# Context, logits, routing weights and maxima turned in 32x32 blocks by VectorE and laid out by DMA

## The chip, the cores and the metric

One core of a Trainium2 chip (trn2) runs the whole program. The metric is the device time of one execution in microseconds; lower is better. Engines are named as the profile names them: PE is TensorE (PEld its weight loads), DVE is VectorE, ACT is ScalarE, POOL is GpSimd, SP is SyncE, which here issues every DMA.

## What is computed

The layer is a residual sum of an attention branch and a routed mixer branch over `x` of shape 8 x 1024 x 256, both fed by the same layer norm:

```python
xn = _layernorm(x)
x = x + attn(xn) + ffn(xn)
# attn: 16 heads of 16; heads 0..3 causal over all keys, heads 4..15 causal over a window of 64
scores = einsum('bhqd,bhkd->bhqk', q, k) * HEAD_DIM ** -0.5
ctx = einsum('bhqk,bhkd->bhqd', softmax(masked scores), v) ; attn = ctx @ w_out + b_out
# ffn: two branches (fwd and inverse) of 8 experts of rank 64
prod = einsum('btd,kdr->btkr', Q, V) * cumsum(einsum('btd,kdr->btkr', K, W), axis=1)
h = gelu(Q @ router_w1.T + router_b1); logits = h @ router_w2.T + router_b2 + expert_bias
weights = softmax(logits)
out = (einsum('btkr,kdr->btd', prod * weights[..., None], U) + weights @ b) / n_valid
ffn = (fwd + alpha_bi * inv) @ W_O.T
```

## The kernel before

**Chunks.** The 8 sequences are cut into 16 chunks of 512 tokens (`C`), two for each sequence; a chunk with an even number is the first half of its sequence and has fewer key tiles in the global heads. For every chunk a list of stages is written out by hand (`plan.stages`), and each of the five engine programs walks the same list in the same order and does its part of each stage. So every engine and SP's queue are strictly in the order of the list, and a stage that waits on one engine holds up all that stands behind it there. Nothing is scheduled at run time. The eight PSUM banks are handed out by turns: a stage on PE waits with `take` until the last user's contents have been read (`bank_read`).

**One chunk** goes through three phases on PE:
- *experts and peaks*: for each of 8 expert pairs `x` (xV), `c` (the cumulated yW), `product`, `mix` (into banks 0 and 1), woven with `lpeak` and `gpeak`: the raw scores, of which DVE takes the row maxima in 128-wide blocks (`peak`, `block_peak`). `found` splits the maxima in three bf16 parts, `rows` turns them on PE, ACT copies them (`peak_f`), SP writes them to DRAM and reads them back as three extra rows under the queries `QS`. `open` starts banks 0 and 1 with the bias rows times the routing weights `WT`; it comes right after the second expert pair's `c`.
- *local*: `lscore` and `lav` for the local heads in three groups of four (`grp` 1 to 3), woven with the next chunk's `turn` (token transpose, split in XH and XL), `sums`, and `parts` (the K and Q projections of the next chunk). For `parts` ACT writes the first bf16 part and DVE the other two (L1256, L1259, L1261). Then four `hidden` stages (the router's first layer, Gelu on ACT, banks 2 and 3 in turn).
- *global*: `gscore` and `gav` for the four global heads, woven with the next chunk's first `x` and `c`, `logits`, `gates`, `gate_parts`, `norm`, `values`; then `weight_rows`, two more `x`, and `finish`, the output projection into banks 0 and 1.

**What is turned on PE now.** `lav` and `gav` leave the context with channels on partitions, one extra row being the softmax sum. For each group ACT copies the bank (`cin`, L1125), PE turns it (`cout`, L913), DVE divides (L1375, L1377) into `ctok`; after the last group PE turns `ctok` back (`cparts`, L922), ACT and DVE split it in `PH` (L1131) and `PL` (L1384), and `finish` multiplies. The logits are copied by ACT (L1043), turned on PE (`gates`, L728), softmaxed by DVE; the weights go to DRAM and come back broadcast (`weights_d`, `wide`), and their three bf16 parts (`wstack`) are turned on PE (`weight_rows`, L737) and copied by ACT into `WT` (L1056).

Of the kernel before, what the change touches and what calls it, by code (L numbers as in the profile page):

```python
# [12 lines left out]
P = 128  # L13
# [56 lines left out]
def mixer_layer(  # L70
# [19 lines left out]
    HALF = C // 2  # L90
    HE_SLOTS = 6
# [14 lines left out]
    VW = HD + 1  # L106

# [73 lines left out]
    def add_cout(ch, grp):  # L181
        add("cout", ch, grp, uses=["bank4", f"craw{grp % 2}"])
# [13 lines left out]
    def add_lav(ch, grp, half):  # L196
        add("lav", ch, grp, half, uses=["bank7"] if half == 0 else [])
        where["lav", ch, grp, half] = [where["lscore", ch, grp, half, pair][1] for pair in range(2)]
        if half == 1:
            add("cin", ch, grp)  # L200
# [4 lines left out]
    def add_gav(ch, j, half):  # L205
        add("gav", ch, j, half, uses=["bank4"] if (j, half) == (0, 0) else [])
        where["gav", ch, j, half] = [where["gscore", ch, j, half, pair][1] for pair in range(2)]
        if (j, half) == tiles(ch % NC)[-1]:
            add("cin", ch, 0)
# [15 lines left out]
    def local_groups(ch):  # L225
# [4 lines left out]
        for n, (grp, half) in enumerate(units):  # L230
# [5 lines left out]
            if n > 2 and half:  # L236
                order[-1].append((add_cout, ch, grp - 1))
# [24 lines left out]
    def add_finish(ch):  # L262
        add("finish", ch, uses=["phl0", "phl1"])
# [24 lines left out]
    def add_gates(ch):  # L288
        add("gates", ch, uses=["bank7"])

    def add_rows(ch, which):
        add("rows", ch, which, uses=["bank4"])
# [67 lines left out]
    add("logits", 0, uses=["bank7", "craw0"])  # L360
# [3 lines left out]
    add("gates", 0, uses=["bank7"])  # L364
# [8 lines left out]
    add("weight_rows", 0, uses=["bank7"])  # L373
    add_open(0)

    for ch in range(CHUNKS):
# [4 lines left out]
        run(experts[0] + peaks[0])  # L381
        weave(experts[1:split], peaks[1:])
# [26 lines left out]
        if nxt:  # L409
            first_x, first_c = ([(add, ch + 1, 0, part) for part in range(2)] for add in (add_x, add_c))  # L410
            run(first_x + order[0] + first_c)
            add("logits", ch + 1, uses=["bank7", "craw0"])
# [14 lines left out]
        for k in range(DB):  # L427
            add_on("cparts", ch, k, uses=[score_use()])
# [3 lines left out]
        add_finish(ch)  # L432

    ctx = ExitStack()
    with ctx:
# [22 lines left out]
        l_bias = sb("l_bias", [P, 2])  # L458
        inv_n = sb("inv_n", [P, ST])
# [25 lines left out]
        weights_t = sb("weights_t", [P, T * 32])  # L485
# [10 lines left out]
        gate = sb("gate", [P, 4, T, 2 * KE])  # L496
        gsum = sb("gsum", [P, 4, T * 2])
        wstack = sb("wstack", [P, T, KSTK], BF16)
# [4 lines left out]
        positions = sb("positions", [P, ST], I32)  # L503
        peak = sb("peak", [P, T, NH])
        peak_rest = sb("peak_rest", [P, T, NH])
        block_peak = [sb(f"block_peak{c}", [P, T, NG, (c + 1) * T]) for c in range(NC)]
        peak_t = [sb(f"peak_t_{n}", [P, T, 3 * k], BF16) for n, k in (("local", NL), ("global", NG))]
        peak_f = sb("peak_f", [3 * NL, C], BF16)
        craw = sb("craw", [P, 2, C])
        ctok = sb("ctok", [P, T, D])  # L510
        cinv = sb("cinv", [P, 2, T, 4])
        logit_f = craw[:, 0, :]
# [4 lines left out]
        weights_d = nc.dram_tensor("weights_d", (2 * KE, C), F32, kind="Internal").ap()  # L517
        xr = x.rearrange("n (c t p) d -> n c p t d", c=NC, t=T)
# [5 lines left out]
        def raw(shape):  # L524
# [7 lines left out]
        rU = [t_[:, :, :].rearrange("p t d -> p (t d)").rearrange("p (b k) -> p b k", b=DB) for t_ in (xt, ctok)]  # L532
# [10 lines left out]
                [[WT[0:1, 0:D], WT[0:1, D:2 * D], peak_f[0:1, 0:D]]]  # L543

        def column(k):
# [12 lines left out]
        craw_read = [sem(f"craw{i}_read") for i in range(2)]  # L558
# [4 lines left out]
        peak_turned = [sem(f"peak_turned{i}") for i in range(2)]  # L563
# [6 lines left out]
        logits_ps, gate_max, gate_exp, gate_split, gate_turned = (sem(n) for n in ("logits_ps", "gate_max", "gate_exp", "gate_split", "gate_turned"))  # L570
# [4 lines left out]
            sem(n) for n in ("lpeaks_ps", "gpeaks_ps", "lscores_ps", "gscores_ps", "ctx_turned", "ctx_hi", "out_ps"))  # L575
        dve_step, pool_step, blank, cleared, selected, readied = (sem(n) for n in ("dve_step", "pool_step", "blank", "cleared", "selected", "readied"))
# [14 lines left out]
        N_RAW = [11, 5, 8, 5, 1]  # L591
# [62 lines left out]
        def tensor_program(e):  # L654
# [12 lines left out]
            for stage in plan.stages:  # L667
# [47 lines left out]
                elif kind == "logits":  # L715
# [3 lines left out]
                    for j in range(2 * DB):  # L719
                        k = where["hidden", ch, j][1]  # L720
                        e.matmul(PS[32 * j:32 * j + KE, 7, :], W2[:, j % DB, :], HE[:, k, :], start=True, stop=True,
                                 skip_group_check=True).then_inc(he_read[k])

                elif kind == "gates":
                    ch, = key
                    take(7, *stage)
                    for t in range(T):
                        ins = e.transpose(psum(7, lo=t * P, hi=(t + 1) * P), logit_f[:, t * P:(t + 1) * P], ident[:, :])  # L728
                    ins.then_inc(craw_read[0])

                elif kind == "weight_rows":
                    ch, = key
# [991 lines left out]
```

## Time and profile before

| | us |
|---|---|
| median of 3 runs (lowest, highest) | 1515.61 (1514.74, 1518.65) |
| profiled execution, its own time | 1516.97 |
| its span in the trace | 1515.3 |
| mean granted TensorE clock, share of full | 0.996 |
| PE busy | 1425.3 (94%) |
| DVE busy | 882.5 (58%) |
| ACT busy | 852.4 (56%) |
| POOL busy | 575.5 (38%) |

The profile is read from PE: it is busy in nearly every slice, so a microsecond taken from its instruction stream is a microsecond of the span, unless PE then waits for something. The trace repeats with the pair of chunks, some 180 us; times in it are given from the span's start.

### The profile page before, as it was taken

What the parts mean: (1) busy time and instruction counts of PE and PEld (TensorE: products, weight loads), DVE (VectorE), ACT (ScalarE), POOL (GpSimd) and SP (SyncE); (2) the same over time, 40 slices, a digit from 0 to 9 for tenths busy, and PEclk for the clock granted to TensorE, in tenths of its full rate; (3) what the DMA queues carried; (4) which work ended last, traced back from release to release, by engine and by line L of the source; (5) the groups of instructions that cost most, each with busy time, mean ns of one, the idle gap of its engine ahead of it and who ended that gap; (6) DMA issues with size and microseconds to landing.
All of it is one profiled execution on the core that took longest, in us unless ns stands there. A gap on an engine that the chain in (4) does not pass through costs nothing.

```text
span 1515.3 us, 36826 instructions
## 1 busy us (share of the span) xinstructions
PE 1425.3 (94%) x14977; PEld 1072.4 (71%) x14977; DVE 882.5 (58%) x1935; ACT 852.4 (56%) x1512; POOL 575.5 (38%) x663
## 2 busy tenths in 40 slices
PE   5999999999999999999999999999999999999997
PEld 4577775867758686686857777586775868678673
DVE  6676773556645675465755577356664567546451
ACT  3446557474665547565474645647466563756544
POOL 1044351444425343352424435143442524335241
PEclk9999999999999999999999999999999999999999
DMA  9322507253251625317053350615325162531600
GB/s 226 81 77 75 145 23 170 65 121 118 64 144 32 156 82 120 102 39 187 31 141 96 83 144 30 162 60 121 118 73 136 32 165 73 120 102 40 174 30 15
DMA packets 153789, 150.56 MB, mean 99 GB/s; under 512 B 28468, under 2 KB 136885, under 8 KB 153573
## 3 DMA queue, kind: packets, MB, share of 16 engines
q1 hardware_dynamic: 153620, 148.22, 37.7%
q8 instruction: 118, 1.93, 0.5%
q14 instruction: 51, 0.41, 0.1%
HBM read 106.98 MB, written 34.87 MB: 94 GB/s over the span
## 4 chain that ended last, share of the span: by engine, by line
PE 75%; DVE 11%; ACT 8%; issue 5%; POOL 1%; DMA 0%; ACTq 0%; POOLq 0%; DVEq 0%
PE PS L660 35%; PE PS L781 11%; PE PS L815 3%; PE PS L932 3%; PE PS L801 3%; PE PS L901 3%; PE PS L869 3%; PE PS L883 3%; ACT HE L1116 2%; PE PS L913 2%; PE PS L987 2%; PE PS L845 2%; ACT HE L1108 2%; DVE block_peak L1292 2%; DVE PL L1384 1%
## 5 line engine op out<-in xcount | busy, mean ns | idle before, releaser
L1547 POOL TENSOR_TENSOR PL<-prod,PH 128x512 fp32r<-128x512 f32 x128 | 164.7, 1287 | 215.1 <-ACT PH L1078 215.1
L1542 POOL TENSOR_TENSOR prod<-prod,rest 128x512 f32<-128x512 f32 x96 | 123.3, 1287 | 265.1 <-ACT prod L1068 146.0
L660 PE MATMUL PS<-XH,WH 128*128 128x512 f32 x512 | 218.3, 426 | 4.5 <-DVE XL L1232 1.9
L1292 DVE TENSOR_REDUCE block_peak<-PS 128x4 f32<-128x512 f32 x288 | 181.0, 684 | 54.2 <-PE PS L815 54.2
L660 PE MATMUL PS<-XL,WH 128*128 128x512 f32 x512 | 203.7, 398 | 0.0
L660 PE MATMUL PS<-XH,WL 128*128 128x512 f32 x512 | 203.2, 397 | 0.0
L1078 ACT ACTIVATE PH<-prod 128x512 fp32r<-128x512 f32 x128 | 80.8, 631 | 209.6 <-DVE prod L1365 209.5
L1525 POOL TENSOR_SCALAR_AFFINE_SELECT HE<-HE 128x256 f32<-128x256 f32 x128 | 51.0, 411 | 347.9 <-ACT HE L1116 345.3
L1116 ACT ACTIVATE HE<-PS 128x512 f32<-128x512 f32 (+1 forms) x320 | 159.7, 552 | 24.8 <-PE PS L883 22.6
L1068 ACT ACTIVATE prod<-PS 128x512 f32<-128x512 f32 x128 | 76.1, 594 | 125.3 <-PE PS L660 114.9
L1285 DVE TENSOR_REDUCE peak<-PS 128x4 f32<-128x512 f32 x192 | 120.6, 682 | 41.1 <-PE PS L801 41.1
L1365 DVE TENSOR_TENSOR prod<-PS,prod 128x512 f32<-128x512 f32 x128 | 88.2, 689 | 87.8 <-PE PS L660 85.1
L781 PE MATMUL PS<-UH,PH 128*128 128x256 f32 x512 | 132.2, 293 | 0.0
L781 PE MATMUL PS<-UL,PH 128*128 128x256 f32 x512 | 125.5, 279 | 0.0
L660 PEld LDWEIGHTS PS<-XH,WH 128*128 128x128 f32 x512 | 96.9, 189 | 29.3 <-DVE rest L1256 3.6
L660 PEld LDWEIGHTS PS<-XH,WL 128*128 128x128 f32 x512 | 96.7, 189 | 23.4
L660 PE MATMUL PS<-CH,WH 128*128 128x512 f32 x256 | 108.9, 425 | 0.7 <-DVE prod L1365 0.7
L1108 ACT ACTIVATE HE<-PS 128x512 f32<-128x512 f32 x192 | 103.4, 591 | 10.5 <-PE PS L845 10.5
L660 PEld LDWEIGHTS PS<-XL,WH 128*128 128x128 f32 x512 | 97.3, 190 | 14.3
L883 PEld LDWEIGHTS PS<-area 99*128 99x128 bf16 x640 | 41.4, 97 | 93.0 <-ACT HE L1116 55.8
L883 PE MATMUL PS<-area 99*128 99x256 bf16 (+1 forms) x640 | 99.6, 265 | 8.1 <-ACT HE L1116 3.9
L660 PE MATMUL PS<-CH,WL 128*128 128x512 f32 x256 | 101.8, 398 | 0.0
(196 smaller groups left out, 3142.3 us busy)
## 6 DMA issues: line engine op xcount, KB each, us to landing
parts_d<-area SPq DMA_DIRECT2D x32, 768.0 KB, 5.1
area<-parts_d SPq DMA_DIRECT2D x128, 192.0 KB, 8.4
rest<-weights_d SPq DMA_DIRECT2D x192, 128.0 KB, 2.9
area<-parts_d SPq DMA_DIRECT2D x32, 576.0 KB, 8.4
tok<-in_L_attn_x_dram SPq DMA_DIRECT2D x16, 512.0 KB, 6.3
xt<-in_L_attn_x_dram SPq DMA_DIRECT2D x16, 512.0 KB, 4.2
wide<-weights_d SPq DMA_DIRECT2D x64, 128.0 KB, 3.0
out_dram<-xt SPq DMA_DIRECT2D x16, 512.0 KB, 3.7
```

What stands on the lines that cost most here:

```text
L660: ins = e.matmul(ps, a, b, start=first and k == 0, stop=last and k == n - 1, skip_group_check=True)
L781: ins = e.matmul(out_half(t), (PH, PL)[part][:, h, t * P:(t + 1) * P], u[:, j, :], start=False, stop=False, skip_group_check=True)
L883: ins = e.matmul(psum(i, lo=HALF * a + lo, hi=HALF * (a + 1)), KG[0:KSTK, g, j * P:(j + 1) * P], QS[0:KSTK, g, half * HALF + lo:(half + 1) ...
L1068: e.activation(prod[:, j % 3, :], psum(2), ACT.Copy).then_inc(bank_read[2])
L1078: e.activation(PH[:, h, :], prod[:, j % 3, :], ACT.Copy).then_inc(phi)
L1108: e.activation(HE[:, k, :], psum(i), ACT.Exp, scale=SCALE).then_inc(bank_read[i])
L1116: e.activation(two(HE[:, k, :], lo), two(psum(i), lo), ACT.Exp, scale=SCALE).then_inc(bank_read[i])
L1285: e.tensor_reduce(peak[:, t, NG + 4 * grp:NG + 4 * (grp + 1)], psum(i).rearrange("p (a k) -> p a k", a=4), AX_X, ALU.max).then_inc(bank_re ...
L1292: e.tensor_reduce(block_peak[ch % NC][:, t, :, j], psum(i).rearrange("p (a k) -> p a k", a=4), AX_X, ALU.max).then_inc(bank_read[i])
L1365: e.tensor_tensor(prod[:, r, :], psum(3), prod[:, r, :], ALU.mult).then_inc(bank_read[3])
L1542: e.tensor_tensor(prod[:, j % 3, :], prod[:, j % 3, :], wide[j % WIDE], ALU.mult).then_inc(weighed)
L1547: e.tensor_tensor(PL[:, j % 2, :], prod[:, j % 3, :], PH[:, j % 2, :].bitcast(F32), ALU.subtract).then_inc(plo)
```

## The change

No operand of the main stream is turned on PE any more. DVE turns 32x32 blocks in place (`e.transpose`); what has to move between partition groups moves by DMA, or is absorbed in the order of weight rows.
- *Context*: `cin`, `cout` and `cparts` go. DVE turns the bank itself into `craw` (new stage `ctx`), divides into `ctok` (still in blocks), and turns `ctok` back (`cturn`) before ACT's copy to `PH`; DVE's `crest` makes `PL`. `w_out` is loaded in the matching row order. `lav` uses bank 7 and bank 4 in turn.
- *Finish* is in two halves: `finish` 0 (groups 1 and 2) near the end of the global phase, `finish` 1 after the next chunk's first product and first three peaks.
- *Logits*: eight 256-wide matmuls for four 512-wide; DVE turns the bank (L728 and L1043 go) and adds the bias.
- *Weights*: DVE splits them in three, turns all at once (`weights_t`); ACT casts to `weights_b`; SP writes them to a new DRAM tensor `rows_d` in four DMAs, waits, and reads them back into `WT` in three. `open` waits for these (`rows_in`).
- *Maxima*: DVE turns them, and SP writes 4 DMAs instead of 1 before the read.

```diff
-    def add_cout(ch, grp):
-        add("cout", ch, grp, uses=["bank4", f"craw{grp % 2}"])
+    def add_ctx(ch, grp):
+        add("ctx", ch, grp)
...
         add_lav(ch, NL // 4, 1)
+        add("cturn", ch, 0)
         if nxt:
             add("keep", ch + 1)
             add("stacks", ch + 1, "local")
-            add_hidden(ch + 1, 0)
-            add_hidden(ch + 1, 1)
-        add_cout(ch, NL // 4)
-        if nxt:
-            add_hidden(ch + 1, 2)
-            add_hidden(ch + 1, 3)
+            for j in range(2 * DB):
+                add_hidden(ch + 1, j)
+        add("crest", ch, 0)
...
+        side.append([(add_finish, ch, 0)])
         weave(order, side)
         if nxt:
             add("stacks", ch + 1, "global")
-            add("weight_rows", ch + 1, uses=["bank7"])
-        add_cout(ch, 0)
+            add("weight_rows", ch + 1)
...
-        for k in range(DB):
-            add_on("cparts", ch, k, uses=[score_use()])
+        add("cturn", ch, 1)
...
-        add_finish(ch)
+        add("crest", ch, 1)
...
# ScalarE
-                elif kind == "cin":
...
-                    e.activation(craw[:, r, :], psum(cb), ACT.Copy).then_inc(bank_read[cb])
-
-                elif kind == "cparts":
+                elif kind == "cturn":
                     ch, k = key
-                    q.wait_ge(ctx_turned, DB * ch + k + 1)
+                    q.wait_ge(ctx_turned, nth(*stage))
                     q.wait_ge(phl_read[k], use(f"phl{k}", "mix", ch, 6 + k, 1))
-                    e.activation(PH[:, k, :], psum(where[stage][0]), ACT.Copy).then_inc(ctx_hi)
+                    e.activation(PH[:, k, :], cturned, ACT.Copy).then_inc(ctx_hi)
...
# VectorE
+                    e.transpose(craw[:, 1, :], psum(cb)).then_inc(bank_read[cb])
+                    q.wait_ge(bank_read[cb], use(f"bank{cb}", *(("lav", ch, grp, 0) if grp else ("gav", ch, 0, 0))))
+                    q.step(e.reciprocal(cinv[:, :], raw_t[:, :, HD]))
+                    q.wait_step()
+                    q.step(e.tensor_tensor(ctok[:, k, :].rearrange("p (b e) -> p b e", e=32)[:, :, half * HD:(half + 1) * HD], raw_t[:, :, 0:HD],
+                                           cinv[:, :].unsqueeze(2).to_broadcast([P, C // 32, HD]), ALU.mult))
...
+                    e.transpose(cturned, ctok[:, k, :]).then_inc(ctx_turned)
...
# SyncE
+                elif kind == "weight_rows":
+                    ch, = key
+                    q.wait_ge(rows_cast, ch + 1)
+                    q.wait_ge(rows_in, 16 * 3 * ch)
+                    for w in range(2):
+                        for h in range(2):
+                            row = 32 * (2 * w + h)
+                            e.dma_start(rows_d[:, KE * w:KE * (w + 1), h * HALF:(h + 1) * HALF], weights_b[row:row + 3 * KE, :]).then_inc(rows_out, 16)
+                    q.wait_ge(rows_out, 16 * 4 * (ch + 1))
...
+                    for n, lo, hi in ((0, 0, 3), (1, 3, 5), (2, 5, 6)):
+                        e.dma_start(WT[2 * KE * lo:2 * KE * hi, :], rows_d[n:n + 1].to_broadcast([hi - lo, 2 * KE, C])).then_inc(rows_in, 16)
```

**ACT at the end of the local phase.** `area` is written by the last `parts`, the table load is Gelu's, and `HE<-PS,r_bias` are the four Gelus of `hidden`. Before:

```order
L1108 ACTIVATE HE<-PS 128x512 [waits he4_read,lscores_ps]
L1010 ACTIVATE area<-PS,q_bias 128x512 [waits parts_ps]
L1125 ACTIVATE craw<-PS 128x512 [waits craw1_read,he4_read]
L1032 ACT_TABLE_LOAD [waits he5_read]
L1032 ACTIVATE HE<-PS,r_bias 128x512 [waits hidden_ps] x2
```

Now:

```order
L1058 ACTIVATE HE<-PS 128x512 [waits he4_read,lscores_ps]
L981 ACTIVATE area<-PS,q_bias 128x512 [waits parts_ps]
L1072 ACTIVATE PH<-craw 128x512 [waits split0_read,ctx_turned]
L1003 ACT_TABLE_LOAD [waits he5_read]
L1003 ACTIVATE HE<-PS,r_bias 128x512 [waits hidden_ps]
```

In the place of a copy that waited for PE alone stands the copy to `PH`, which waits for DVE (`ctx_turned`), ahead of the table load and the Gelus.

**DVE in the local phase**, from the second `parts` of K to the end. Before:

```order
L1256 SCALAR_TENSOR_TENSOR rest<-PS,k_bias,area 128x512 [waits carried,clo,part1]
L1259 CAST area<-rest 128x512 [waits bank3_read_out]
L1261 TENSOR_TENSOR area<-rest,area 128x512 [waits dve_step]
L1256 SCALAR_TENSOR_TENSOR rest<-PS,q_bias,area 128x512 [waits part3,part1]
L1259 CAST area<-rest 128x512 [waits bank2_read_out]
L1375 RECIPROCAL cinv<-PS 128x16 [waits craw0_read]
L1377 TENSOR_TENSOR ctok<-PS,cinv 128x4x64 [waits dve_step]
L1276 MEMSET area 99x12x32 [waits lscores_ps]
```

Now:

```order
L1196 SCALAR_TENSOR_TENSOR rest<-PS,k_bias,area 128x512 [waits carried,clo,part1]
L1199 CAST area<-rest 128x512 [waits bank3_read_out]
L1319 STREAM_TRANSPOSE craw<-PS 128x512 [waits he4_read]
L1321 RECIPROCAL cinv<-craw 128x16 [waits bank4_read_out]
L1323 TENSOR_TENSOR ctok<-craw,cinv 128x16x16 [waits dve_step]
L1196 SCALAR_TENSOR_TENSOR rest<-PS,q_bias,area 128x512 [waits part3,part1]
L1319 STREAM_TRANSPOSE craw<-PS 128x512 [waits he2_read]
L1321 RECIPROCAL cinv<-craw 128x16 [waits bank7_read_out]
L1323 TENSOR_TENSOR ctok<-craw,cinv 128x16x16 [waits dve_step]
L1331 STREAM_TRANSPOSE craw<-ctok 128x512 [waits dve_step]
L1216 MEMSET area 99x12x32 [waits lscores_ps]
```

Group 2's turning and division now stand ahead of the Q parts, and behind the last part stand group 3's and the turning back of `ctok`.

**SP at the end of a chunk's global phase** (`area<-parts_d` are the global stacks, `rest` and `wide` the broadcast weights). Before:

```order
L1626 DMA area<-parts_d 48x4x512
L1626 DMA area<-parts_d 16x4x512 x3
L1680 DMA rest<-weights_d 64x512 x4
L1680 DMA wide<-weights_d 64x512 x2
L1685 DMA out_dram<-xt 128x4x256
```

Now:

```order
L1587 DMA area<-parts_d 48x4x512
L1587 DMA area<-parts_d 16x4x512 x3
L1637 DMA rows_d<-weights_b 3x8x256 x4
L1643 DMA WT<-rows_d 48x1x512
L1643 DMA WT<-rows_d 32x1x512
L1643 DMA WT<-rows_d 16x512
L1658 DMA rest<-weights_d 64x512 x4
L1658 DMA wide<-weights_d 64x512 x2
L1663 DMA out_dram<-xt 128x4x256
```

Seven DMAs, with a wait for the first four between, stand between the stacks and the next weights.

## Rows read from the trace of the kernel before

**Rows 1.** The page: PE's busy time, share and instructions

```profile
PE 1425.3 (94%) x14977; PEld 1072.4 (71%) x14977; DVE 882.5 (58%) x1935; ACT 852.4 (56%) x1512; POOL 575.5 (38%) x663
```

**Rows 2.** Groups on PE: count, busy us, mean ns, idle before, releaser

```profile
L913 PE MATMUL PS<-ident,craw 128*128 128x128 f32 x256 | 41.1, 283 | 7.2 <-ACT craw L1125 7.2
L922 PE MATMUL PS<-ident,ctok 128*128 128x128 f32 x128 | 17.0, 276 | 1.9 <-DVE ctok L1377 1.9
```

**Rows 3.** Timeline, end of a local phase: start, us, engine, line, idle before

```profile
759.71 0.75 DVE L1256 SCALAR_TENSOR_TENSOR rest<-PS,k_bias,area 128x512 f32<-128x512 f32 x1 [1.47 <-ACT area L1010]
...
767.34 1.28 ACT L1032 ACT_TABLE_LOAD   x1
...
768.46 0.69 DVE L1261 TENSOR_TENSOR area<-rest,area 128x512 bf16<-128x512 f32 x1
...
768.64 0.69 ACT L1032 ACTIVATE HE<-PS,r_bias 128x512 f32<-128x512 f32 x1
...
769.88 0.48 PE L660 MATMUL PS<-XH,WH 128*128 128x512 f32 x1
```

**Rows 4.** Groups on DVE and ACT that price the new operations

```profile
L1346 DVE STREAM_TRANSPOSE weights_t<-gate 128x128 f32<-128x128 f32 x16 | 5.0, 311 | 0.5
L1375 DVE RECIPROCAL cinv<-PS 128x16 f32<-128x16 f32 x64 | 16.3, 255 | 126.2 <-PE PS L913 126.2
L1377 DVE TENSOR_TENSOR ctok<-PS,cinv 128x256 f32<-128x256 f32 x64 | 27.2, 424 | 2.2
L1131 ACT ACTIVATE PH<-PS 128x512 fp32r<-128x512 f32 x32 | 17.4, 597 | 3.7 <-PE PS L922 3.7
L1292 DVE TENSOR_REDUCE block_peak<-PS 128x4 f32<-128x512 f32 x288 | 181.0, 684 | 54.2 <-PE PS L815 54.2
```

**Rows 5.** Timeline, `gates` in the global phase

```profile
778.04 0.66 PE L728 MATMUL PS<-ident,craw 128*128 128x128 f32 x4 [0.35 <-ACT craw L1043]
778.63 0.63 PE L901 MATMUL PS<-HE,Va 128*17 128x256 f32 x8
```

**Rows 6.** Timeline, end of the same global phase

```profile
797.47 0.43 PE L737 MATMUL PS<-ident_b,wstack 128*99 128x128 bf16 x4
...
798.69 0.48 PE L660 MATMUL PS<-XH,WH 128*128 128x512 f32 x1
...
800.37 0.60 ACT L1068 ACTIVATE prod<-PS 128x512 f32<-128x512 f32 x1 [1.66 <-PE PS L660]
...
801.03 0.50 PE L660 MATMUL PS<-XH,WH 128*128 128x512 f32 x1
```

**Rows 7.** SP's queue (SPq) and `open`: stacks before an odd and an even chunk's `open`

```profile
797.01 5.12 SPq L1626 DMA_DIRECT2D area<-parts_d  x8
810.19 0.61 PE L748 MATMUL PS<-bias_rows,WT 99*128 99x256 bf16 x4
886.54 5.81 SPq L1626 DMA_DIRECT2D area<-parts_d  x8
892.25 0.61 PE L748 MATMUL PS<-bias_rows,WT 99*128 99x256 bf16 x4
```

**Rows 8.** SP's queue: a small write to DRAM and the read that waits for it

```profile
848.70 0.29 SPq L1654 DMA_DIRECT2D peak_d_global<-peak_f  x1
850.05 0.23 SPq L1656 DMA_DIRECT2D area<-peak_d_global  x1
```

**Rows 9.** Busy time by window: PE, PEld, DVE, ACT, POOL (count), granted clock, DMA share, GB/s

```profile
30.00:31.00 1.00, 0.00 (x0) 0.00 (x0) 1.00 (x1) 0.00 (x0) 0.00 (x0) 1.00 1.09 383
33.00:34.00 1.00, 1.00 (x6) 1.00 (x5) 0.00 (x0) 0.91 (x3) 0.00 (x0) 0.50 0.39 92
35.00:36.00 1.00, 0.85 (x4) 0.77 (x5) 0.00 (x0) 0.10 (x1) 0.00 (x0) 0.84 0.23 53
```

**Rows 10.** Timeline at the start: the first `open` and the first `weigh`

```profile
82.31 0.61 PE L748 MATMUL PS<-bias_rows,WT 99*128 99x256 bf16 x4 [0.69 <-ACT WT L1056]
...
86.88 2.52 POOL L1542 TENSOR_TENSOR prod<-prod,rest 128x512 f32<-128x512 f32 x2 [67.59 <-DMA rest<-weights_d]
```

More of the change, by code:

```diff
@@ L288, in add_gates @@
     def add_gates(ch):
-        add("gates", ch, uses=["bank7"])
+        add("gates", ch)
     def add_rows(ch, which):
-        add("rows", ch, which, uses=["bank4"])
+        add("rows", ch, which)
     def add_norm(ch, order):
@@ L517, in mixer_layer @@
         weights_d = nc.dram_tensor("weights_d", (2 * KE, C), F32, kind="Internal").ap()
+        rows_d = nc.dram_tensor("rows_d", (3, 2 * KE, C), BF16, kind="Internal").ap()
         xr = x.rearrange("n (c t p) d -> n c p t d", c=NC, t=T)
@@ L718, in tensor_program @@
                     take(7, *stage)
[L719 to L732, printed above, removed]
-                    q.wait_ge(gate_split, ch + 1)
-                    take(7, *stage)
-                    wt_ps = PS[0:KSTK, 7, :].bitcast(BF16)
-                    for t in range(T):
-                        ins = e.transpose(wt_ps[:, t * P:(t + 1) * P], wstack[:, t, :], ident_b[:, :])
-                    ins.then_inc(gate_turned)
+                    for b in range(DB):
+                        for w in range(2):
+                            k = where["hidden", ch, DB * w + b][1]
+                            for h in range(2):
+                                row = 32 * (2 * w + h)
+                                ins = e.matmul(PS[row:row + KE, 7, 0:HALF], W2[:, b, :], HE[:, k, h * HALF:(h + 1) * HALF], start=(b == 0),
+                                               stop=(b == DB - 1), skip_group_check=True)
+                            ins.then_inc(he_read[k])
                 elif kind == "open":
                     ch, = key
-                    q.wait_ge(bank_read[7], use("bank7", "weight_rows", ch))
+                    q.wait_ge(rows_in, 16 * 3 * (ch + 1))
+                    q.wait_ge(ones_set, 3)
                     if ch == 0:
@@ L817, in tensor_program @@
                     ins.then_inc(gpeaks_ps)
-                elif kind == "rows":
-                    ch, which = key
-                    n = (NL, NG)[which]
-                    q.wait_ge(peak_split[which], ch + 1)
-                    take(4, *stage)
-                    ps = PS[0:3 * n, 4, :].bitcast(BF16)
-                    for t in range(T):
-                        ins = e.transpose(ps[:, t * P:(t + 1) * P], peak_t[which][:, t, :], ident_b[:, :])
-                    ins.then_inc(peak_turned[which])
                 elif kind == "lscore":
@@ L1365, in vector_program @@
                     e.tensor_tensor(prod[:, r, :], psum(3), prod[:, r, :], ALU.mult).then_inc(bank_read[3])
-                elif kind == "cout":
+                elif kind == "ctx":
                     ch, grp = key
-                    r, tb = grp % 2, 4
-                    raw_t = psum(tb).rearrange("p (t g e) -> p t g e", t=T, g=4)
-                    q.wait_ge(craw_read[r], use(f"craw{r}", *stage))
+                    k, half = CTX_AT[grp]
+                    cb = ctx_bank(grp)
+                    raw_t = craw[:, 1, :].rearrange("p (b e) -> p b e", e=32)
+                    if grp:
+                        q.wait_ge(*av_read(*[s for s in plan.stages if s[0] == "lscore" and s[1:3] == (ch, grp)][-1]))
+                    else:
+                        q.wait_ge(*av_read(*last_global(ch)))
@@ L1404, in vector_program @@
                     q.wait_ge(selected, N_SELECT)
-                    q.step(e.tensor_copy(inv_n[:, :], positions[:, :]))
+                    q.step(e.tensor_copy(inv_n[:, :, :], positions[:, :, :]))
+                    for g in range(1, 4):
+                        rows = slice(32 * g, 32 * (g + 1))
+                        q.wait_step()
+                        q.step(e.tensor_scalar(inv_n[rows, :, :], inv_n[rows, :, :], float(HALF * (g % 2) - 32 * g), None, ALU.add))
                     q.wait_step()
-                    q.step(e.reciprocal(inv_n[:, :], inv_n[:, :]))
+                    q.step(e.reciprocal(inv_n[:, :, :], inv_n[:, :, :]))
                     for i in (4, 7):
@@ L1579, in sync_program @@
                             load(dst[:, b, :].rearrange("p (k r) -> p k r", k=KE), src[:, b * P:(b + 1) * P, :].rearrange("k p r -> p k r"), 2)
-                    load(rOUT, w_out.rearrange("(b p) d -> p b d", p=P), 3)
+                    for grp in range(NH // 4):
+                        k, half = CTX_AT[grp]
+                        for g in range(4):
+                            row = 32 * g + HD * half
+                            load(rOUT[row:row + HD, k, :], w_out[HD * (4 * grp + g):HD * (4 * grp + g + 1), :], 3)
                     for dst, src in zip(rU, (U_fwd, U_inv)):
@@ L1680, in sync_program @@
                         e.dma_start(wide[j % WIDE][R * k:R * (k + 1), :], weights_d[2 * j + k:2 * j + k + 1, :].to_broadcast([R, C])).then_inc(wide_in[j % WIDE], 16)
-                elif kind == "finish":
-                    ch, = key
+                elif kind == "finish" and key[1] == 1:
+                    ch, k = key
                     q.wait_ge(bank_read[1], use("bank1", "open", ch))
```

306 lines of the change are left out of this document (140 added, 166 removed).

## Prediction

> **What bounds the kernel now.** I read the page first: PE is busy 94% of the span [rows 1], at a mean granted clock of 0.996. So the kernel is PE's instruction stream, and two questions remain: what a removed instruction occupied in that stream, and whether PE has to wait for whoever takes its work over. For the first I read the groups of the turning instructions and what PE idled before them [rows 2], then the timeline around them, since neighbouring matmuls overlap and a mean of 283 ns overstates what one occupies. For the second I read the timeline of all engines at the end of the local phase [rows 3], because there DVE, which looks idle on average (58%), works without a gap: its L1256, L1259, L1261 follow each other from 759.71 until the last ends at 768.46 + 0.69 = 769.15. That is the place into which the change puts most of its new DVE work.
>
> **The change part by part.** I go by the steady pair of chunks around 750 to 900 us, and count the time at which PE starts a given instruction.
>
> *What goes from PE.* Of `cout` a group of four occupies about 0.4 (four of the 283 ns, pipelined: the next instruction starts 0.35 to 0.41 later); three of them lie in the local phase and are counted there. `gates` occupies 0.59 (778.04 to 778.63) and was waited for 0.35, together 0.94 [rows 5]. `weight_rows` and the last `cout` with its wait lie between 797.47 and 798.69: 1.22 [rows 6]. The `rows` of the local maxima occupy some 0.35 and are waited for some 0.25 on average, 0.6; `found` on DVE grows by a turning of 0.31 and by wider operands, of which I let 0.2 reach PE, so 0.4 is gained. `finish` loses a wait of 0.25.
>
> *What gains nothing.* `cparts` are eight turnings of the kind above, some 0.8 in all [rows 2], and the matmul behind them starts at 801.03. That belongs to `x` 2, which takes bank 2, and this is free only when ACT has copied `x` 1: 800.37 + 0.60 = 800.97 [rows 6]. Without `cparts` PE stands idle until the same moment. The 0.8 is a cover that goes; its gain is zero.
>
> *The local phase.* This is the term that decides. The price of DVE's new turning of 512 columns is in no row. Below, the 128-column one takes 311 ns [rows 4], so 0.31 is the floor; above, four times that in full is 1.24. The DVE operations on 512 columns of PSUM take 0.684 and those on 256 0.424 [rows 4], which is one column each ns or so plus a start; 311 for 128 lies on that line. I take 0.70. A `ctx` is then 0.70 + 0.26 + 0.42, with gaps 1.42.
>
> DVE's unbroken stretch begins when ACT has written the first K part, 759.71 now, and some 0.6 earlier with one `cout` and one wait fewer in front: 759.1. It lasts 9.44 now, with one reciprocal and multiply in it (0.67). In its place comes group 2's `ctx`: 759.1 + 9.44 - 0.67 + 1.42 = 769.3. Behind it `ctx` of group 3, 770.7, and `cturn`, 0.70 with a gap: 771.5. (Group 1's `ctx` falls in the idle time ahead of the stretch, 1.47 [rows 3], and costs nothing; if DVE were late there, it would be another 1.4.) Only now does ACT make `PH`, 0.60 [rows 4], to 772.1. Behind that wait, in ACT's order, stand the table load, 1.28, and the first Gelu, 0.69 [rows 3]: 774.1. The third `hidden` takes bank 2, which this Gelu frees. It starts at 769.88 now [rows 3] and at 774.1 then: 4.3 later, although two and a half groups of transposes are gone from the stream ahead of it. PE, which is done with the second `hidden` at about 769.6, idles some 4.5.
>
> This happens in the 15 chunks that have a successor. Per chunk so far: 4.3 - 0.94 - 1.22 - 0.25 - 0.4 = +1.5.
>
> *The clock.* PE has no idle time that long after the start now. At the start it has one of 2.5 us (nothing runs in 30 to 31), with little work around it; about 2 us after it the granted clock is 0.50, that is 1.2 instead of 2.4 GHz, for some 3.3 us until it is back in 35 to 36 [rows 9]. While it is halved PE does half the work: 1.7 lost. I take it that 2 of 3 of the idle times of 4.5 bring this on: 1.1 a chunk. The Trainium skill (TensorE: Matmul & The Clock Gate, Why this matters for your kernels) likewise warns of idle gaps between bursts of matmuls, after which TensorE is back at its low clock; by it every chunk would pay, and the sum below would be 8 us higher.
>
> *`open` waits for DMAs.* SP issues the stacks until 797.01 + 5.12 = 802.13 and 886.54 + 5.81 = 892.35; `open` is at 810.19 and 892.25 [rows 7]. Behind the stacks now come four writes, a wait, three reads. A small write issues in 0.29 and the read that waits for it starts 1.35 after the write did [rows 8], so a hop beyond the issue is 1.06. A stack's DMA issues in 5.12 / 8 = 0.64. The new ones are small, but of 24 short rows each: I take 0.35, between 0.29 and 0.64. Writes 1.4, hop 1.1, reads 1.05, landing some 1.4: 4.9 after the stacks (4.2 to 7.0 by the bounds). Before an even chunk's `open` there are 8.1 us of room, and PE is later, not earlier: nothing is waited for. Before an odd chunk's there is none: the rows are in at 892.35 + 4.9 = 897.3. PE would come at 892.25 + 4.3 - 0.94 - 1.22 - 0.25 = 894.1, with the clock term 895.2. So 2.1 to 3.2, and I take 2.3, in 8 chunks. This holds if SP comes to the stacks no later than now; it is held up before them by the weights' way through DRAM, whose DMAs queue behind the local stacks. The Trainium skill (DMA: Bandwidth & Descriptors, the two cost components at its start) gives about 2 us as the fixed cost of a DMA; [rows 8] show a shorter hop, 1.35 with its issue. By the page's figure each of the two hops would be 0.6 longer and the sum 10 us higher.
>
> *The start.* The first `open`, at 82.31 now, stands directly behind `weight_rows` in the list, and in SP's queue a `wide` that waits for the first `weigh` stands ahead of the rows. That `weigh` starts at 86.88 [rows 10]; I take 86.0 (the weights' writes are fewer pieces), done 87.3, two `wide` issues 88.5, rows 4.9 and somewhat more: 93.5. So +11, once (7 to 13).
>
> *The last chunk* has no `hidden`: it gains its `cout`s, and half of `finish` goes from the tail: -5.
>
> Sum: 15 x 1.5 = 22; -0.4 for the sixteenth's maxima; clock 15 x 1.1 = 17; `open` 8 x 2.3 = 18; start 11; last chunk -5. Together +63. Against the profiled execution's 1516.97 that is 1580; its own median of runs lies 1.4 lower, so **1578 us**.
>
> **The rivals.**
> *A: faster, DVE is early enough.* If PE didn't wait at the third `hidden`, the transposes would be gone for good: 0.94 + 1.22 + 0.25 + 0.4 + about 1.5 in the local phase, 4.3 a chunk, 69 in all, less what `open` then waits more (PE 4.3 earlier than now in every odd chunk, so 897.3 against some 889, 8 x 8 = 64, unless SP is earlier too) and the 11 of the start, with 5 gained at the end. Taken so, all but the last gain is eaten by `open`, and the time is 1516, no change; with SP 3 earlier as well, since the weights' writes are fewer pieces, it is about 1492. What decides is the chain 759.1 to 774.1: it must end 4 us earlier, at 770. A turning at the floor of 0.31 shortens it by only 3 x 0.39 = 1.2, a table load that had been done before by 1.28, and both together don't reach it. For it speaks only the average, DVE at 58%; against it the row-by-row order.
> *B: slower, but the clock holds.* The idle times leave the clock at full: 1578 - 17 + 8 (`open` waits 1 more) = 1569.
> *C: slower, and more.* The turning is nearer 1.1: 3 x 0.4 = 1.2 a chunk more, the clock falls every time (0.6 more), the rows need 7.0 instead of 4.9: 18 + 9 + 17 = 44 more, 1622.
> *D: no change.* `open` never waits, the clock holds, and the turning is at its floor: 22 - 18 + 11 - 5 = +10, 1526; it needs the gains elsewhere to be some 10 larger to come out at 1515.
>
> **How the numbers follow.** The forecast with its clock and `open` terms holds 0.40, B 0.22, C 0.13, D's neighbourhood above 1520 0.08, within 0.3% (A with SP no earlier, and the rest of D) 0.05, A 0.12. No change means within 0.3%, 4.5 us, about what these runs can tell. The likeliest case's own range is 1545 to 1610. The range that leaves out 2 in 10 runs from 1518, below which A and most of D lie, to 1625, the end of C. Faster 0.12, same 0.05, slower 0.83.
>
> **What would show it.** In the profile after: PE idle before a weight matmul of `hidden` (L671), released by an ACT Gelu, 15 times some 4.5 us; ACT idle before `PH<-craw` (L1072) for DVE's turning, and the table load right behind it; DVE's groups of 512-column turnings at about 0.70; the granted clock at 0.5 in short stretches behind those idle times; idle time before L748, released by the DMA `WT<-rows_d`, in odd chunks and in the first; none before L748 in the other even ones. An idle time before the second `x` (L671) of 0.8 released by ACT's copy shows that `cparts` gained nothing. PE's busy time should fall by about 60 to 70 us. The prediction is wrong if the turning is far below 0.3, if PE's wait at `hidden` is under 2 us, or if the stages before the local phase were themselves waiting in a way that a later PE repairs.

## The result, and the profile after

| | before | after |
|---|---|---|
| median (lowest, highest), 4 runs each | 1515.43 (1514.74, 1518.65) | 1680.79 (1675.77, 1682.54) |
| profiled execution: own time, span | 1516.97, 1515.3 | 1675.77, 1674.1 |
| mean granted clock | 0.996 | 0.951 |

The ratio is 1.108 (95% interval 1.105 to 1.111): slower, as forecast, but 165 us slower where 63 were forecast, and outside the range. The page of after, engines and then the chain that ended last; it answers to [rows 1]:

```profile
PE 1421.3 (85%) x14465; PEld 1059.4 (63%) x14465; DVE 999.2 (60%) x2066; ACT 792.5 (47%) x1400; POOL 586.2 (35%) x663
PE 53%; DVE 16%; SPq 10%; ACT 8%; issue 6%; DMA 5%; POOL 1%; ACTq 0%; DVEq 0%; POOLq 0%
```

PE has 512 matmuls fewer and is busy almost as long. The waits of PE after (engine, line, released by: us in total, times, longest):

```profile
PE PS L748 <- DMA WT<-rows_d: 81.3, 16, 15.8
PE PS L671 <- ACT HE L1003: 64.5, 15, 4.3
PE PS L904 <- DVE PL L1336: 14.2, 9, 3.7
PE PS L836 <- ACT PS L1051: 13.5, 25, 0.7
PE PS L689 <- DVE tok L1165: 11.4, 1, 11.4
PE PS L671 <- ACT prod L1030: 10.3, 15, 0.7
```

The first two, `open` and the third `hidden`, are new and hold 146 of the 159 us that the span grew. The place of the second, where [rows 3] stood, in the timeline of after (start, us, engine, line, operation; in brackets the idle time and its releaser):

```profile
757.22 0.71 DVE L1331 STREAM_TRANSPOSE craw<-ctok 128x512 f32<-128x512 f32 x1
...
757.96 0.63 ACT L1072 ACTIVATE PH<-craw 128x512 fp32r<-128x512 f32 x1 [5.36 <-DVE craw L1331]
758.61 1.28 ACT L1003 ACT_TABLE_LOAD   x1
...
759.90 1.27 ACT L1003 ACTIVATE HE<-PS,r_bias 128x512 f32<-128x512 f32 x2
...
760.64 0.50 PE L671 MATMUL PS<-XH,WH 128*128 128x512 f32 x1 [4.30 <-ACT HE L1003]
```

This is the forecast chain link by link: the back-turning, the copy to `PH`, the table load, the Gelu, bank 2. The other place is `open`, which answers to [rows 7]:

```profile
782.13 6.49 SPq L1587 DMA_DIRECT2D area<-parts_d  x8
...
788.72 3.02 SPq L1637 DMA_DIRECT2D rows_d<-weights_b  x4
...
792.98 1.85 SPq L1643 DMA_DIRECT2D WT<-rows_d  x3
...
796.93 1.03 PE L748 MATMUL PS<-bias_rows,WT 99*128 99x256 bf16 x4 [6.80 <-DMA WT<-rows_d]
```

From the end of the stacks, 788.62, to `open` it is 8.3 us. And the granted clock behind a wait of each kind (windows as in [rows 9]; PE's busy share is the first number behind the window's length):

```profile
760.00:761.00 1.00, 0.36 (x2) 0.31 (x3) 0.00 (x0) 1.00 (x2) 0.00 (x0) 1.00 0.99 288
761.00:762.00 1.00, 1.00 (x4) 0.80 (x3) 0.00 (x0) 0.17 (x1) 0.00 (x0) 0.56 1.09 384
763.00:764.00 1.00, 1.00 (x4) 0.81 (x3) 0.00 (x0) 0.69 (x1) 0.00 (x0) 0.50 1.13 243
```

```profile
796.00:797.00 1.00, 0.07 (x1) 0.08 (x2) 0.00 (x0) 0.00 (x0) 0.00 (x0) 0.50 0.68 131
801.00:802.00 1.00, 1.00 (x19) 0.83 (x15) 0.87 (x2) 0.14 (x1) 0.00 (x0) 0.50 0.67 230
802.00:803.00 1.00, 1.00 (x5) 0.82 (x6) 1.00 (x2) 1.00 (x2) 0.00 (x0) 0.96 0.01 3
```

The clock is at 0.50 (1.2 for 2.4 GHz) for some 3.4 us from shortly after the wait at `hidden` ends, and until 802 behind the longer one at `open`, where it had begun to fall during the wait (0.92 in 791 to 792) and where `open`'s own four matmuls take 1.03 instead of 0.61.

**Where the 159 us are.** I summed one minus the granted clock, times PE's busy share, over all windows of 1 us: PE loses 58.8 us of work to the clock in after, 4.7 in before (below I call this the clock sum). So PE's work at full clock fell from 1420.6 to 1362.5, by 58: the change does take that off PE. The clock gives back 54 of it. PE's time outside its busy time grew from 90.0 to 252.8, by 163: `open` 81.3, `hidden` 64.5, `finish` 14.2 for 5.3, the second `x` 10.3 for nothing, and so on, less some 20 of waits that went with the transposes. -58 + 54 + 163 = 159.

### The profile page after: what moved, and what is told of

It is laid out like the page before. It is cut to its first block, busy times and chain, and to the rows that moved or that the text cites. A ratio compares the mean times of both kernels' runs of the same rounds, so it can differ in the third digit from the quotient of the medians.

```text
span 1674.1 us, 35980 instructions
## 1 busy us (share of the span) xinstructions
PE 1421.3 (85%) x14465; PEld 1059.4 (63%) x14465; DVE 999.2 (60%) x2066; ACT 792.5 (47%) x1400; POOL 586.2 (35%) x663
## 4 chain that ended last, share of the span: by engine, by line
PE 53%; DVE 16%; SPq 10%; ACT 8%; issue 6%; DMA 5%; POOL 1%; ACTq 0%; DVEq 0%; POOLq 0%
PE PS L671 25%; PE PS L782 10%; SPq L1587 5%; PE PS L816 4%; DVE rest L1196 3%; PE PS L875 3%; DMA WT<-rows_d 2%; ACT HE L1066 2%; DVE area L1201 2%; SPq L1637 2%; DVE area L1199 2%; PE PS L893 2%; DMA rows_d<-weights_b 2%; PE PS L802 2%; PE PS L958 2%
## 5 line engine op out<-in xcount | busy, mean ns | idle before, releaser
L671 PE MATMUL PS<-XH,WH 128*128 128x512 f32 x512 | 233.3, 456 | 86.4 <-ACT HE L1003 64.5
L671 PE MATMUL PS<-XH,WL 128*128 128x512 f32 x512 | 213.9, 418 | 0.0
L671 PE MATMUL PS<-XL,WH 128*128 128x512 f32 x512 | 213.8, 418 | 0.0
L671 PEld LDWEIGHTS PS<-XH,WH 128*128 128x128 f32 x512 | 104.7, 204 | 136.0 <-ACT HE L1003 71.0
L782 PE MATMUL PS<-UH,PH 128*128 128x256 f32 x512 | 141.1, 306 | 0.0
L782 PE MATMUL PS<-UL,PH 128*128 128x256 f32 x512 | 133.8, 292 | 0.0
L1046 ACT ACTIVATE PS<-peak_mask_l 128x512 f32<-128x512 bf16 x144 | 86.3, 602 | 74.0 <-DVE peak L1225 73.7
L671 PEld LDWEIGHTS PS<-XH,WL 128*128 128x128 f32 x512 | 103.2, 202 | 25.2
L671 PEld LDWEIGHTS PS<-XL,WH 128*128 128x128 f32 x512 | 105.6, 206 | 16.0
L875 PE MATMUL PS<-area 99*128 99x256 bf16 (+1 forms) x640 | 101.4, 267 | 10.4 <-ACT HE L1066 7.3
L1319 DVE STREAM_TRANSPOSE craw<-PS 128x512 f32<-128x512 f32 x64 | 45.5, 710 | 104.8 <-PE PS L893 100.2
```

The costliest lines, as they stand in the source:

```text
L671: ins = e.matmul(ps, a, b, start=first and k == 0, stop=last and k == n - 1, skip_group_check=True)
L782: ins = e.matmul(out_half(t), (PH, PL)[part][:, h, t * P:(t + 1) * P], u[:, j, :], start=False, stop=False, skip_group_check=True)
L875: ins = e.matmul(psum(i, lo=HALF * a + lo, hi=HALF * (a + 1)), KG[0:KSTK, g, j * P:(j + 1) * P], QS[0:KSTK, g, half * HALF + lo:(half + 1) ...
L1046: e.activation(psum(i).rearrange("p (a k) -> p a k", a=4), local_peak_mask(*of[1:3]), ACT.Copy).then_inc(seeded)
```

## The experiments

My theory was now: two waits of position (ACT's `PH` copy ahead of the Gelus; the rows' DMAs last in SP's queue), each with its fall of the clock behind it. The rival was that an engine or a queue is short of throughput, so that a wait moved out of one place turns up in another. "Expected" texts are those written ahead of each run; "the kernel before" measured 1514.4 to 1518.4 beside all of them. The numbers of the lines shift a little from kernel to kernel: `open` is L747 to L751, `hidden` L670 to L674.

**1. The Gelus ahead of the copy to `PH`.**

```diff
         add_lav(ch, NL // 4, 1)
-        add("cturn", ch, 0)
         if nxt:
...
                 add_hidden(ch + 1, j)
+        add("cturn", ch, 0)
         add("crest", ch, 0)
```

> The changed kernel with the local half's back-turning and its copy to PH put behind the four hidden stages, so that ACT's Gelus stand ahead of the copy. Theory 1 (ACT waits for DVE's context chain and PE waits for ACT): the 15 waits of 4.3 us before the third hidden stage go (64.5 us), and so do the 15 falls of the clock behind them (some 1.7 us each, 25 us): 1681 - 90 = 1591 us, 1575 to 1610. Rival (DVE is what bounds the local and global phase, so that its chain only comes to the surface elsewhere, at crest, rest or PL): the waits turn up again before other stages and the time stays within 20 us of 1681.

Measured: 1618.47 us (1614.43 to 1620.64), 62 under the changed kernel, where 90 were expected, and over the expected range. PE's waits in it:

```profile
PE PS L748 <- DMA WT<-rows_d: 115.9, 16, 16.4
```

The waits for the Gelu are gone from the list, all 64.5 us, and the clock sum falls from 58.8 to 33.0, the 25 expected. The waits at `open`, though, grew from 81.3 to 115.9, all but 0.6 of it in the odd chunks (8.8 to 11.2 where they were 5.2 to 7.0). Ahead of the stacks and the rows SP has its `wide` reads, which wait until the weights' own four writes to DRAM have landed. SP's wait for these, first in the changed kernel, then here:

```profile
SPq L1658 <- DMA weights_d<-weights_t: 17.9, 16, 1.9
SPq L1658 <- DMA weights_d<-weights_t: 74.3, 16, 6.2
```

SP issues the weights' writes sooner, but then stands some 5 us for them instead of 1, and everything behind comes hardly sooner. Theory 1 holds for `hidden`, and the rival has a part too: not in DVE, at `crest` or `rest`, where I had put it, but in SP's queue. More than half of the 64.5 had been hiding time that `open` needs. It is what the prediction had named as a condition: "the weights' way through DRAM, whose DMAs queue behind the local stacks".

**2. The rows' DMAs earlier in SP's queue.**

```diff
-            side += [[(add_values, ch + 1, 0)], [(add_values, ch + 1, 1)]]
+            side += [[(add_values, ch + 1, 0), (add, "weight_rows", ch + 1)], [(add_values, ch + 1, 1)]]
...
             add("stacks", ch + 1, "global")
-            add("weight_rows", ch + 1)
```

> The changed kernel with the stage that writes the weight rows to DRAM and reads them back moved from behind the global stacks to beside the first half of values, some 10 to 20 us earlier in the order. Theory 1 (PE waits at open for transfers that are only queued too late): of the 81 us that PE waits at open 65 go and the first, 16 us, stays; with the clock that falls behind these waits (some 35 us of PE's work) 1681 - 100 = 1581 us, 1560 to 1610. Rival (SP's queue is what bounds: seven DMAs of 0.6 to 0.75 us issue and their own wait of 2 us hold up Vs and the stacks behind them): waits at the scores and the values of the next phase take the place of those at open, and the time stays above 1640.

Measured: 1608.42 us (1606.84 to 1610.18), 72 under the changed kernel. PE's waits:

```profile
PE PS L670 <- ACT HE L1002: 64.5, 15, 4.3
PE PS L747 <- DMA WT<-rows_d: 15.9, 1, 15.9
```

Only the first `open` still waits. The stacks and `Vs` behind the moved DMAs are not late for anything: no wait for them is in the list. The clock sum fell from 58.8 to 44.5 only, 14 and not 35. In the changed kernel the stretches of low clock behind `open` hold 21.6, and they are gone; but those behind the unchanged waits of 4.30 at `hidden` grew from 28.5 to 32.5, since 8 of the 15 are now twice as long, where 4 were (3.4 us of clock lost for 1.7; of PE's work 2.2 to 3.0 for 1.4 to 1.7). Elsewhere the loss grew by 3. The same wait brings on either size; what decides between them no run shows.

**3. Both.**

> Both moves together: Gelus ahead of the copy to PH, and the weight rows beside the first half of values. Theory 1: the two effects add, 1681 - 90 - 100 = 1491 us, 1470 to 1515, so at or under the kernel before (1515), since PE's own work at full clock is 58 us less. Rival (DVE bounds, with 999 us busy and its steps longer beside GpSimd): the sum is less than the parts, over 1530.

Measured: 1539.94 us (1534.80 to 1543.63), ratio to the kernel before 1.015 (1.013 to 1.018). The two parts add up (62 + 72 = 134, measured 141), but the time is 49 above the 1491 expected and 25 above the range. It is over the rival's 1530 as well, but not by the rival's mechanism, since the sum isn't less than the parts and no wait for DVE has grown by as much as 1 us. The reason is in one line of PE's waits and in SP's queue before an odd chunk:

```profile
PE PS L747 <- DMA WT<-rows_d: 43.5, 9, 16.0
```

```profile
716.51 1.29 SPq L1627 DMA_DIRECT2D weights_d<-weights_t  x4
722.51 2.42 SPq L1657 DMA_DIRECT2D rest<-weights_d  x4
724.98 1.83 SPq L1657 DMA_DIRECT2D wide<-weights_d  x2
726.92 3.38 SPq L1636 DMA_DIRECT2D rows_d<-weights_b  x4
731.54 1.86 SPq L1642 DMA_DIRECT2D WT<-rows_d  x3
```

PE, no longer held at `hidden`, comes to eight of the `open`s 3.4 us (2.2 to 4.2) before the rows. ACT had `weights_b` ready at 717.03; SP stood from 717.8 to 722.51 at the `wide` reads (`rest<-weights_d` and `wide<-weights_d`), with the ready writes of the rows queued behind them. What it waited for stands in the chain that ended last (start, us, what), and what the DMA engines did meanwhile in the windows (DMA share and GB/s are the last two numbers):

```profile
717.51 4.99 DMA weights_d<-weights_t
```

```profile
719.00:720.00 1.00, 1.00 (x15) 1.00 (x12) 0.83 (x6) 0.78 (x3) 0.25 (x1) 1.00 1.14 198
721.00:722.00 1.00, 1.00 (x18) 0.64 (x11) 0.77 (x4) 0.00 (x0) 0.00 (x0) 1.00 0.08 18
```

The last of the four writes of the weights, 8 KB each, lands only after 5 us. The eight local stacks were issued from 705.81 to 711.84, and the DMA engines are full until nearly 721; that the small writes stand behind the stacks' traffic fits this, but no run took the stacks away. This is the wait of SP that run 2 had hidden behind the other (19.5 us there, 72.6 here).

**4. Fill the wait at `hidden` with matmuls: the clock alone.**

```diff
                     take(i, *stage)
+                    if ch and j == 1:
+                        for _ in range(3):
+                            mms(psum(i), weight_pairs(COL_R + j * P, XH, XL))
                     mms(psum(i), weight_pairs(COL_R + j * P, XH, XL)).then_inc(hidden_ps)
```

> The changed kernel with 18 matmuls more (4.2 us) in the second hidden stage of each chunk but the first, into the bank that this stage fills anyway, so that PE works where it waited for ACT; nothing waits for less or for more. The wait of 4.3 us becomes 0.1 to 0.5. Theory 1 (the clock falls because PE stands still there): the granted clock stays full behind the third hidden stage, and the time falls by 15 x 1.7 = 25 us to 1656 us (1648 to 1668) although 270 matmuls are added. Rival (the clock falls there for another reason, such as the Gelus or the load of the chip): the clock still falls, and the time stays at 1681 or rises by up to 10.

Measured: 1657.12 us (1655.77 to 1663.74), 24 under the changed kernel with 270 matmuls more. Where 761 to 765 above showed 0.50, the windows around and behind the start of the third `hidden` of the same chunk, 752.89 here, now read (and 1.00 on to 757):

```profile
752.00:753.00 1.00, 0.91 (x5) 0.43 (x4) 0.00 (x0) 0.99 (x3) 0.00 (x0) 1.00 0.95 240
753.00:754.00 1.00, 1.00 (x5) 0.81 (x6) 0.00 (x0) 0.53 (x1) 0.00 (x0) 1.00 1.08 385
```

The chain DVE, ACT, Gelu is the same and ends when it did; only PE's standing still is gone, and with it the fall of the clock: the clock sum is 36.9 for 58.8, 22 less. Of the 22 the two profiled executions show 17.5 in the time, since the waits at `open` grew by 3. That the idle time of PE, and nothing else in this place, brings the clock down is shown: neither the Gelus nor the load of the chip do it when PE has work.

**5. What a write costs SP.**

```diff
-                            e.dma_start(rows_d[:, KE * w:KE * (w + 1), h * HALF:(h + 1) * HALF], weights_b[row:row + 3 * KE, :]).then_inc(rows_out, 16)
+                            for n in range(3):
+                                e.dma_start(rows_d[n, KE * w:KE * (w + 1), h * HALF:(h + 1) * HALF], weights_b[row + KE * n:row + KE * (n + 1), :]).then_inc(rows_out, 16)
```

> The changed kernel with each write of the weight rows (24 partitions of 512 B) cut in three of 8 partitions: 12 writes for 4. It measures what SP pays to issue a write. In the changed kernel a write of 24 partitions takes 0.755 us of SP and a write of the weights with 8 partitions 0.33. Theory A (the price grows with the rows that a DMA moves, with a small fixed part): 12 writes of 8 take 12 x 0.33 = 4.0 us, 1.0 more than the 3.02 of now, each wait at open is 1 us longer, and the time is 10 to 25 us over the changed kernel. Rival B (a fixed price for each write to this tensor, 0.755): 12 writes take 9.1 us, each wait is 6 us longer, and the time is 90 us or more over.

Measured once: 1704.23 us, 23 over the changed kernel. SP's queue:

```profile
799.28 4.15 SPq L1638 DMA_DIRECT2D rows_d<-weights_b  x12
804.39 1.97 SPq L1644 DMA_DIRECT2D WT<-rows_d  x3
```

12 writes of 8 rows take 4.15, 0.346 each; 4 of 24 rows take 3.02, 0.755 each. Two points give 0.14 us and 0.0256 for each row: theory A. (A write split in three also has a dimension less, 8 rows for 3x8; these runs don't tell the two apart.) It does not go with the bytes: the weights' writes, 8 rows of 1 KB, take 1.29 for four, 0.32 each. A DMA that is small in bytes (24 rows are 12 KB) is not a cheap one. The line is one of these small writes alone: the reads into `WT`, of 48, 32 and 16 rows, take 0.71, 0.64 and some 0.4, and the reads of 64 rows into `rest` 0.61.

**6. The writes directly behind those of the weights.** On the kernel of run 3 the stage is cut in two; SP's order is then: weights to DRAM, rows to DRAM, `wide` reads, `WT` reads. SP's wait for the last chunk's `WT` reads, ahead of the writes, goes as well.

```diff
         add("gate_parts", ch)
+
+    def add_weight_rows(ch):
+        add("weight_rows", ch)
         for j in range(WIDE):
             add_wide(ch, j)
+        add("row_reads", ch)
...
-            side += [[(add_values, ch + 1, 0), (add, "weight_rows", ch + 1)], [(add_values, ch + 1, 1)]]
+            side += [[(add_values, ch + 1, 0), (add_weight_rows, ch + 1)], [(add_values, ch + 1, 1)]]
```

> Both moves, and the stage of the weight rows cut in two: the four writes to DRAM stand right behind the four of the weights, the reads of the broadcast weights come next, and the three reads into WT behind those, so that the hop from write to read is filled. In the kernel with both moves PE still waits 43.5 us at open: 16.0 in the first chunk and some 3.4 in each of eight others, because SP issues the six broadcast reads (4.2 us) ahead of the writes. Theory 1 (only the place in SP's queue matters): the eight waits go, the first falls by the hop and by part of the writes to about 11 us, and with the clock behind them (some 10 us) 1540 - 27 - 5 - 10 = 1498 us (1485 to 1510), under the kernel before. Rival (the reads of the broadcast weights are late next, since the rows' writes now stand ahead of them): waits of 2 to 3 us at the products, and 1515 to 1540.

Measured: 1505.28 us (1503.21 to 1506.90), ratio to the kernel before 0.993 (0.991 to 0.995). SP before the same chunk as in run 3, then PE's wait:

```profile
697.59 1.30 SPq L1631 DMA_DIRECT2D weights_d<-weights_t  x4
698.93 3.03 SPq L1639 DMA_DIRECT2D rows_d<-weights_b  x4
703.61 2.44 SPq L1663 DMA_DIRECT2D rest<-weights_d  x4
706.09 1.69 SPq L1663 DMA_DIRECT2D wide<-weights_d  x2
707.90 1.93 SPq L1648 DMA_DIRECT2D WT<-rows_d  x3
```

```profile
PE PS L751 <- DMA WT<-rows_d: 11.5, 1, 11.5
```

The writes of the rows stand in the time in which SP waits for those of the weights anyway, the hop to DRAM is covered by the `wide` reads, and the eight waits are gone. The `wide` reads are not late next. The clock sum is 11.5 us.

**7. The first `open` where the others stand.** Only `if j == 1 and ch` becomes `if j == 1` in the order of the experts, and the separate first `open` goes.

> The kernel of the last run but one (both moves, writes ahead), with the first chunk's open where the other chunks have it, behind the second expert pair's c. PE waits 11.5 us there for the first WT, and the clock falls behind it. Some 9.5 us of x, raw scores and c of the second pair then stand ahead of it. Theory 1: the wait falls to about 2 us, and with part of the clock 1505 - 9 - 2 = 1494 us (1490 to 1500). Rival (the products of the first pairs wait for the broadcast weights behind the same reads, so that the wait moves to the second and third x): 1503 to 1507, no change.

Measured: 1495.51 us (1495.01 to 1499.97), ratio 0.987 (0.985 to 0.989). The wait for the rows is down to 0.7:

```profile
PE PS L750 <- DMA WT<-rows_d: 0.7, 1, 0.7
```

PE is busy 1379.8 of 1493.8; its idle time, 114, is still 24 more than before the change, in small pieces such as these:

```profile
PE PS L673 <- ACT prod L1032: 10.3, 15, 0.7
PE PS L818 <- ACT PS L1050: 8.4, 17, 0.8
PE PS L877 <- ACT HE L1068: 7.9, 21, 0.6
```

## Why the prediction was right and wrong

**Right: the chain at `hidden`.** Forecast 15 waits of some 4.5; they are 15 of 4.30. The price without a row, DVE's turning of 512 columns, was taken as 0.70 between 0.31 and 1.24; it is 0.71 (L1319, the group of 64, mean 710 ns; 256 columns take 0.45, 128 take 0.31). Run 1 shows the place: with only the back-turning and its copy moved behind the four `hidden`, all 15 waits go.

**Right: `cparts` gains nothing.** The second `x` now waits 0.7 for ACT's copy, 15 times, 10.3 us: bank 2 set that time before and sets it still.

**Right: what leaves PE.** A fall of 60 to 70 us of PE's busy time was forecast. At full clock it is 58. The page shows 4, and whoever reads only the page misses it, because the clock puts 54 back.

**Wrong: the price of the rows' DMAs.** The step was "I take 0.35, between 0.29 and 0.64 ... 4.9 after the stacks (4.2 to 7.0 by the bounds)". It is 8.3, above the upper bound, by four pieces: writes 0.755 each and not 0.35, +1.6; the hop 1.24 and not 1.1; reads 0.62 each, +0.8; landing 2.1 and not 1.4, +0.7. The piece that counts most is the write. Its bounds came from DMAs that are not of its kind: by run 5 a write of 24 rows costs more than twice one of 8, and the rows of the two DMAs that gave the bounds were not looked at. Even the second line of [rows 7] gives a stack 5.81 / 8 = 0.73, over the bound of 0.64; and seven DMAs of 0.29 with hop and landing are 4.5, not 4.2. That PE would come to the odd `open` 1.8 us behind the stacks, 2.9 with the clock term, was right (1.5 to 3.2, 2.4 on average), so nearly all of the difference between the 2.3 forecast and the 5.2 to 7.0 measured in eight chunks is this price. The rule of the Trainium skill that I had weighed (DMA: Bandwidth & Descriptors, the two cost components at its start: about 2 us fixed for each DMA, a figure that the page gives for DMAs issued from GpSimd, while here SP issues) was nearer than what I took. Counted as I had counted [rows 8], with the issue of the last DMA, the hop is 1.89 and the landing 2.47, where [rows 8] had 1.35; without it they are 1.24 and 2.1.

**Wrong: "before an even chunk's `open` ... nothing is waited for".** Seven waits of 2.0 to 3.2, 17 us. The room behind the stacks is no longer 8.1:

```profile
888.65 5.09 SPq L1587 DMA_DIRECT2D area<-parts_d  x8
893.84 3.02 SPq L1637 DMA_DIRECT2D rows_d<-weights_b  x4
898.11 1.84 SPq L1643 DMA_DIRECT2D WT<-rows_d  x3
...
902.07 0.61 PE L748 MATMUL PS<-bias_rows,WT 99*128 99x256 bf16 x4 [2.10 <-DMA WT<-rows_d]
```

Stacks end at 893.74 and PE is ready at 899.97: 6.2, since `weight_rows`, `cout` and `cparts` have gone from PE between the two; the DMAs need 8.3. I said that PE is "later, not earlier", which is so against the clock on the wall, but SP's start of the stacks waits for PE's scores, so the delay at `hidden` moves both. With my 4.9 it would have been hidden all the same.

**Wrong: the start.** +11 forecast; the first `open` starts at 96.95 where it started at 82.31, +14.6. SP starts the rows' writes at 88.73, where I had 88.5; what failed is again the 4.9.

**Wrong: the clock.** Forecast 17 ("2 of 3 of the idle times of 4.5", 1.7 each). The size of an episode was right for the shorter of the two sizes. The count was not: the clock falls behind all 15 waits at `hidden`, for 28.5 us in all, behind all eight odd `open`s and two of the even ones, 21.6, and a little at both ends. The sum is 54 more than before. The rule of the Trainium skill that I set beside this step (TensorE: Matmul & The Clock Gate, Why this matters for your kernels) was right in the direction that I discounted: by it every chunk pays.

By size, then, of the missing 102 us, 96 between the two profiled executions: the waits at `open` are 81.3 against 18 and 11 forecast, 52; the clock behind `hidden` is 28.5 against 17, 12; the clock behind `open` 22, elsewhere 3. The rest, some 7, is small: `finish` waits 14.2 for `PL` where I had a quarter of a microsecond gained in each chunk, and `x` and `parts` wait where a transpose had filled the time.

**The rivals.** A's mechanism stands, and its arithmetic too: it said that without the wait at `hidden` "all but the last gain is eaten by `open`". Run 1 shows it in part (35 us of 90), and run 6, with SP earlier as well, is the faster case that A named: 1505 and, with the first `open` mended, 1495.5, for A's estimate of 1492. C was right that the clock falls every time and that the rows are dear (7.0, still too little), and wrong in its slower turning; its 1622 is the nearest of the four, without being near. D's 1526 lies above the 1518 under which the prediction puts "most of D", a slip in its range. The theory that DVE's throughput bounds is gone: DVE is busy 992 us in the fastest kernel of all, for 999 in the changed one.

## What to carry to other kernels

Taking transposes off a busy engine pays only if nothing in a fixed order stands behind the slower path: here the same instructions, with three stages in other places, went from 1681 to 1495.5 us, 20 under the kernel before. Ask for each new wait what is queued behind it (here, ACT's Gelus behind a copy; SP's ready writes behind reads that waited for other writes to land), and mend them together, since one wait hides the next. And price a DMA's issue by a DMA with as many rows, and a wait on PE by itself plus the half-clock work behind it.

## What the runs showed of the hardware that was not expected

- Issuing a write to DRAM from SP is no constant: 0.346 us for 8 rows of 512 B, 0.755 for 24 (run 5).
- Writes of 8 KB can take long to land: SP stood some 1 us for the weights' four writes in most chunks of the changed kernel, and 4.3 to 6.2 in 14 chunks of run 1, where they start 4.1 to 5.0 us behind the last issue of the eight local stacks and not 10.4 or more. That the stacks' traffic holds them up fits the DMA share of run 3; no run took it away.
- One and the same wait of PE, 4.30 us, was followed by a stretch of low clock of one of two sizes, 1.7 or 3.4 us of clock lost, in the changed kernel and in run 2.
- DVE's operations whose operands are all in SBUF have no fixed price. L1165, four groups of 128x256, in the changed kernel, where GpSimd works at the same time, and in run 3, where it idles:

```profile
780.54 2.84 POOL L1497 TENSOR_TENSOR prod<-prod,rest 128x512 f32<-128x512 f32 x2 [2.27 <-DMA rest<-weights_d]
...
780.99 3.19 DVE L1165 TENSOR_SCALAR tok<-tok,mv,var 128x256 f32<-128x256 f32 x4
```

```profile
723.21 1.38 DVE L1164 TENSOR_SCALAR tok<-tok,mv,var 128x256 f32<-128x256 f32 x4
```

0.80 against 0.35 for one. The new `ctok` multiply, whose operand came from PSUM before at a steady 424 ns [rows 4], has a mean of 723 ns from `craw` in SBUF (424 to 1362). That GpSimd is the cause fits these rows; no run took it away, so it stays open. The turnings themselves keep their 0.71 from either place (L1319 from PSUM 710, L1331 from SBUF 708).
